# Adjacency product and routed feed-forward on one core: the start, the second expert's loads and the last expert's rows rearranged

## The chip, the cores and the metric

The kernel runs on one core of a Trainium2 chip. The metric is the device time of one execution in microseconds (us); less is better. Engines are named as the profile names them: PE is the matrix engine (PEld its weight loads), DVE the vector engine, ACT the scalar engine, POOL is GpSimd, SP the engine that issues most DMAs (SPq is its queue). Times inside a trace count from the span's start.

## The reference

```python
def _L0_gnn_ref(user_feat, item_feat, adj, W_item, b_item, W_user, b_user):
    h = item_feat @ W_item.T + b_item            # items: 10000 x 128
    b = user_feat @ W_user.T + b_user
    return jax.nn.relu(adj @ h + b)              # adj: 10000 x 10000, 400 MB
...
x = x + _L0_gnn_ref(_layernorm(x, axis=-1), ...)
# feed-forward: layernorm, logits = x @ gate_w + gate_b, softmax, argmax -> one of 8 experts;
# each expert keeps its first C = 1250 * 1.25 = 1563 tokens in order of arrival;
# hmid = relu(buf @ w1 + b1); ybuf = hmid @ w2 + b2; y = ybuf[slot] * prob, 0 for tokens not kept
x = x + _L0_ffn_ref(_layernorm(x, axis=-1)[None], ...)[0]
```

## The kernel before

**Adjacency part.** The 10000 users are cut into 20 blocks of 500 (`BLOCK`), the 10000 items into 78 chunks of 128 and a rest of 16 rows. Chunks go in 20 groups (`SIZES`, 4 chunks each, the last 3). For each group SP loads 128 x 2000 floats of the adjacency (`raw`, a ring of 10, 1 MB a group), ACT rounds it to the matrix engine's reduced format (`a_hi`, `high` at L545, a ring of 4), DVE subtracts to get the rest (`a_lo`, `low` at L746), and PE makes per chunk three products: high part of h by `a_hi` (L1210), low part of h by `a_hi` (L1212), high part of h by `a_lo` (L1221). `high_part(b, q, g)` holds the first two kinds, `low_part` the third, one group later.

**h itself** is made during block 0: `h_chunks(g)` on PE (L1193, float32), `h_bias(g)` on DVE (L724, from PSUM), `h_high(g)` on ACT (L531), `h_low(g)` on DVE (L736). PE runs `h_chunks(g + 2)` ahead of `high_part(0, 0, g)`, and needs `h_hi` and `h_lo` of group g for it. DVE runs `low(g)`, `h_low(g + 1)`, `h_bias(g + 2)` in this order; ACT runs `high(g)`, `h_high(g + 1)`. SP loads the items of group g + 2 behind the adjacency of group g, and waits for `h_chunks(g)` there; what stands behind in SP's queue waits with it.

**Start.** SP loads the constants (`cst`, 302.5 KB), then `item_consts` (the item weights, 128 KB), then items. DVE makes a number of small constants (`set_up` counts to 8), PE multiplies the gate's weights by a matrix of 1/128 (L1347, its mean), DVE subtracts the result (L1013), and only then does PE begin with `h_chunks(0)`.

**Routing.** While block b is multiplied, DVE picks the experts of block b - 2 (`choose`, `pick`, `assign`, `settle`), POOL takes a reciprocal root (`x1_scale` at L1103, `x_scale` at L1099, both on 125 x 4 numbers), and issues indirect DMAs: `scatter` (four of 125 rows, L1111, into the experts' slots `records`) and `pass_on` (L1117).

**Feed-forward.** Each expert's slots go in units of tiles x rows (`RANK_UNITS`): 4, 3, 3 and 3 tiles of mostly 124 rows for the first ranks; 31 units with 101 tiles in all. For unit n: SP loads its records (`load_rec`, a ring of `BODY` = 8), ACT normalizes (`normalize_slots`, L636), PE transposes (`turn_slots`, L1305), ACT and DVE split into high and low, PE multiplies by w1 (`mid`, L1317 to L1319) and w2 (`second`, L1328), ACT adds the bias (`take_y`, L663), PE transposes back (`turn_y`, L1339), DVE scales and adds (`gate_and_add`), and POOL writes each tile to `out` with one indirect DMA (L1178). SP learns from DVE which expert comes next (`order_ready`) and which units need the last block's tokens (`landed`, a value load), and loads w1 (`load_w1`, L451) and w2 (`load_w2`, L457) of each expert. The order around the change is written out by hand: the first units are lines of their own, the rest a loop `step(at)` with fixed lags.

## Time and profile before

| what | value |
|---|---|
| median of 3 runs | 1350.68 us (1349.1 to 1350.9) |
| the profiled execution's own time | 1349.38 us |
| its span | 1347.6 us |
| PE busy | 1308.6 us (97%) |
| DVE busy | 1179.6 us (88%) |
| ACT busy | 941.7 us (70%) |
| POOL busy | 533.2 us (40%) |
| DMA, mean over the span | 328 GB/s |

The span runs from the first to the last recorded instruction; the execution's own time is 1.8 us longer. PE's busy time is modelled from pipelined matmuls, so two products that follow each other at once overlap in it: the pace is read from starts, not from durations.

### The profile page before, as it was taken

How to read it: one execution, taken by the hardware profiler on the slowest of the kernel's cores; microseconds unless marked ns; L12 is line 12 of the kernel's file. 1: busy time of each engine (PE TensorE's matmuls, PEld its weight loads, DVE VectorE, ACT ScalarE, POOL GpSimd, SP SyncE). 2: the span in 40 equal slices, each digit the busy share in tenths (PEclk: the TensorE clock that was granted, in tenths of full speed). 3: DMA queues.
4: the chain of work that ended last, by engine and by line, in shares of the span. 5: the costliest groups of instructions: out<-in, count | busy, mean ns of one | idle time of the engine just before them, and what ended most of it. 6: DMA issues, size and time to landing. Idle time of an engine off the chain costs nothing. (4 is left out here: it accounts for less than half of the span.)

```text
span 1347.6 us, 19376 instructions
## 1 busy us (share of the span) xinstructions
PE 1308.6 (97%) x6026; PEld 1077.9 (80%) x6026; DVE 1179.6 (88%) x1828; ACT 941.7 (70%) x918; POOL 533.2 (40%) x332
## 2 busy tenths in 40 slices
PE   7999999999999999999999999999999999799993
PEld 6888888888888888888888888888888888577772
DVE  7999989898898998989989899898898988577774
ACT  4777767767677676776767768767677676587771
POOL 0001063250431514415134052350532636777887
PEclk9999999999999999999999999999999999899997
DMA  8999999999999999999999999999999995343310
GB/s 322 358 379 407 413 399 398 375 378 386 366 381 370 374 392 367 381 377 371 386 366 376 380 375 374 378 373 385 370 378 379 368 369 226 102 113 91 78 46 4
DMA packets 96743, 441.52 MB, mean 328 GB/s; under 512 B 26601, under 2 KB 34551, under 8 KB 96695
## 3 DMA queue, kind: packets, MB, share of 16 engines
q1 hardware_dynamic: 68815, 417.83, 81.3%
q0 software_dynamic: 21920, 12.86, 3.8%
q10 hardware_dynamic: 5960, 10.24, 2.3%
q8 instruction: 24, 0.39, 0.1%
q14 instruction: 24, 0.20, 0.0%
HBM read 427.77 MB, written 23.83 MB: 335 GB/s over the span
## 5 line engine op out<-in xcount | busy, mean ns | idle before, releaser
L746 DVE TENSOR_TENSOR a_lo<-raw,a_hi 128x2000 fp32r<-128x2000 f32 (+1 forms) x400 | 864.0, 2187 | 76.3 <-ACT a_hi L545 74.4
L545 ACT CAST a_hi<-raw 128x2000 fp32r<-128x2000 f32 (+1 forms) x400 | 724.0, 1827 | 272.6 <-PE bank L1212 170.9
L1210 PE MATMUL bank<-a_hi,h_hi 128*128 128x500 f32 x1560 | 613.3, 393 | 0.7 <-issue 0.7
L1212 PE MATMUL bank<-a_hi,h_lo 128*128 128x500 f32 x1560 | 606.0, 388 | 0.0
L1221 PE MATMUL bank<-a_lo,h_hi 128*128 128x500 f32 x1560 | 418.1, 389 | 0.0
L1210 PEld LDWEIGHTS bank<-a_hi,h_hi 128*128 128x128 f32 x1560 | 293.5, 188 | 59.1 <-issue 1.3
L1221 PEld LDWEIGHTS bank<-a_lo,h_hi 128*128 128x128 f32 x1560 | 293.2, 188 | 58.9
L1212 PEld LDWEIGHTS bank<-a_hi,h_lo 128*128 128x128 f32 x1560 | 294.0, 188 | 56.7
L1103 POOL TENSOR_TENSOR late<-ve,neghalf 125x4 f32<-125x4 f32 x20 | 55.3, 2765 | 620.1 <-DVE ve L763 620.1
L1178 POOL DMA_INDIRECT out<-raw x101 | 138.8, 1374 | 42.0 <-issue 31.3
L1117 POOL DMA_INDIRECT out<-late,kept_out x76 | 134.7, 1772 | 23.1 <-issue 23.1
L1111 POOL DMA_INDIRECT records<-late,slot x80 | 134.2, 1678 | 22.9 <-issue 22.9
L1328 PE MATMUL bank<-raw 128*128 128x372 f32 (+5 forms) x248 | 90.3, 507 | 0.9 <-ACT raw L663 0.9
L1328 PEld LDWEIGHTS bank<-raw 128*128 128x128 f32 x248 | 45.7, 194 | 28.9 <-issue 15.4
L1099 POOL TENSOR_TENSOR xrs<-xve,neghalf 125x4 f32<-125x4 f32 x20 | 28.9, 1446 | 93.6 <-DVE xve L763 93.2
L655 ACT ACTIVATE raw<-bank,raw 128x372 f32<-128x372 f32 (+5 forms) x124 | 63.6, 592 | 1.6 <-PE bank L1319 1.3
L636 ACT ACTIVATE raw<-raw 124x128 f32<-124x128 f32 (+4 forms) x101 | 42.2, 492 | 7.0 <-DMA raw<-records 7.0
L663 ACT ACTIVATE raw<-bank,raw 128x372 f32<-128x372 f32 (+5 forms) x31 | 18.3, 592 | 39.2 <-PE bank L1328 37.0
L1317 PE MATMUL bank<-h_lo 128*128 128x372 f32 (+5 forms) x124 | 45.6, 368 | 0.0
L1318 PE MATMUL bank<-h_lo 128*128 128x372 f32 (+5 forms) x124 | 42.7, 344 | 0.0
L1319 PE MATMUL bank<-h_lo 128*128 128x372 f32 (+5 forms) x124 | 42.5, 343 | 0.0
L1041 DVE TENSOR_TENSOR raw<-bank,raw 124x384 f32<-124x384 f32 (+5 forms) x31 | 18.3, 591 | 22.9 <-PE bank L1339 22.6
(147 smaller groups left out, 830.3 us busy)
## 6 DMA issues: line engine op xcount, KB each, us to landing
raw<-adj_m SPq DMA_DIRECT2D x380, 1000.0 KB
raw<-adj_m SPq DMA_DIRECT2D x20, 500.0 KB
xT<-x_t ACTq DMA_DIRECT2D x20, 250.0 KB
late<-items_t SPq DMA_DIRECT2D x19, 256.0 KB, 4.9
xb<-x ACTq DMA_DIRECT2D x20, 224.0 KB
raw<-records SPq DMA_DIRECT2D x14, 191.8 KB
raw<-w SPq DMA_DIRECT2D x8, 258.5 KB
raw<-w SPq DMA_DIRECT2D x8, 256.0 KB
```

Of the source, the lines that this page charges most:

```text
L545: last = nc.scalar.copy(a_hi[:, g % HI_RING, 0:m], raw[:, g % RAW, 0:m])
L655: nc.scalar.activation(hm[:, n % HM_RING, f, 0:m], ps_mid[f][:, 0:m], ACT.Relu, bias=bias_of(n, f)).then_inc(hm_ready, 1)
L746: last = v.tensor_tensor(a_lo[:, g % RAW, 0:m], raw[:, g % RAW, 0:m], a_hi[:, g % HI_RING, 0:m].bitcast(F32), ALU.subtract)
L1103: p.tensor_tensor(rec[:, q, :, C_RSTD:C_RSTD + 1], ve[:, :].unsqueeze(2), neghalf[:, :].unsqueeze(2), ALU.pow).then_inc(rstd_ready, 1)
L1111: p.indirect_dma_start(rec_d, bass.IndirectOffsetOnAxis(ap=slot[:, q, j:j + 1], axis=0), rec[:, q, j, :], None, bounds_check=SLOTS - 1, oo ...
L1117: p.indirect_dma_start(out, bass.IndirectOffsetOnAxis(ap=kept_out[:, q, j:j + 1], axis=0), rec[:, q, j, 0:HID], None, bounds_check=USERS - ...
L1178: p.indirect_dma_start(out, bass.IndirectOffsetOnAxis(ap=tokq[0:slot_rows(n), n % YRING, j:j + 1].bitcast(U32), axis=0), yout[0:slot_rows( ...
L1210: nc.tensor.matmul(acc[q][:, 0:BLOCK], h_hi[:, k * HID:(k + 1) * HID], a, start=(k == 0), stop=False)
L1212: last = nc.tensor.matmul(acc[q][:, 0:BLOCK], h_lo[:, k * HID:(k + 1) * HID], a, start=False, stop=False)
L1221: last = nc.tensor.matmul(acc[q][:, 0:BLOCK], h_hi[:, k * HID:(k + 1) * HID], a_lo[:, g % RAW, c * BLOCK:(c + 1) * BLOCK], start=False, st ...
L1317: nc.tensor.matmul(to, w1_hi[:, w, cols], x2q_hi[:, n % 2, 0:m], start=True, stop=False)
L1328: last = nc.tensor.matmul(ps_y[:, 0:m], wb2[:, w, f * HID:(f + 1) * HID], hm[:, n % HM_RING, f, 0:m], start=(f == 0), stop=(f == FC - 1))
```

## The change

- **Start.** SP loads `item_consts` first and `cst` only behind the items of group 2. The first adjacency group is loaded and rounded in two halves, and PE begins with the first half. PE first makes 8 products of a constant tile (`WARM`) that nothing uses. The small constants, the gate's mean product and its subtraction move into block 0 and block 1.
- **Order in block 0.** PE runs `high_part(0, 0, g)` ahead of `h_chunks(g + 2)`; SP loads the items of group g + 1, not g + 2, behind adjacency group g. `h_low` moves from DVE to POOL.
- **Second expert.** SP loads records of units 4 and 5 ahead of w1 and w2, units 6 and 7 follow, and w1 of the third expert comes behind them, each expert's number loaded when it is needed. `normalize_slots(4)` on ACT stands behind `take_y(2)`, `turn_slots(4)` on PE behind `turn_y(2)`, `gate_and_add(2)` ahead of the loop.
- **Last block.** POOL runs `x1_scale(19)` behind the third of the four scatters of block 18, not behind all four.
- **Last expert.** Its first two units have 124 rows, not 122.

```diff
-RANK_UNITS = (WHOLE,) * 6 + (((4, 124), (3, 124), (3, 124), (2, 125)), ((4, 122), (4, 122), (3, 102)))
+RANK_UNITS = (WHOLE,) * 6 + (((4, 124), (3, 124), (3, 124), (2, 125)), ((4, 124), (4, 124), (3, 102)))
...
+                    half = 2 * BLOCK if fixed and b == 0 and g == 0 else 0
+                    if half:
+                        sp.dma_start(raw[:, 0, 0:half], adj_b[:, 0:half],
+                                     max_dma_last_dim=16384).then_inc(first_half_loaded, 16)
...
-                    if fixed and b == 0 and g + 2 < GROUPS:
-                        load_items(g + 2)
+                    if fixed and b == 0 and 2 <= g + 1 < GROUPS:
+                        load_items(g + 1)
+                        if g == 1:
+                            sp.dma_start(cst[:, :], consts).then_inc(consts_loaded, 16)
...
-            sp.dma_start(cst[:, :], consts).then_inc(consts_loaded, 16)
-            sp.dma_start(gnn[:, 0:2 * HID], item_consts).then_inc(consts_loaded, 16)
+            sp.dma_start(gnn[:, 0:2 * HID], item_consts).then_inc(item_consts_loaded, 16)
...
                     store_last_x1()
                     sp.wait_ge(order_ready, 2)
                     expert.append(sp.value_load(order_rest[0:1, 1:2], min_val=0, max_val=EXPERTS - 1))
-                    load_w1(1)
-                    enough[n] = landed(n)
+                    enough[n] = enough[n + 1] = landed(n + 1)
...
                 load_rec(n)
-                if n == UNITS_E:
+                if n == UNITS_E + 1:
+                    load_w1(1)
                     load_w2(1)
-                    expert.extend(sp.value_load(order_rest[0:1, m:m + 1], min_val=0, max_val=EXPERTS - 1)
-                                  for m in range(2, EXPERTS))
+                if n == BODY - 1:
+                    expert.append(sp.value_load(order_rest[0:1, 2:3], min_val=0, max_val=EXPERTS - 1))
                     load_w1(2)
-                    for m in range(UNITS_E + 1, BODY):
-                        enough[m] = landed(m)
...
+                half = 2 * BLOCK if isinstance(b, int) and b == 0 and g == 0 else 0
+                if half:
+                    act.wait_ge(first_half_loaded, 16)
+                    nc.scalar.copy(a_hi[:, 0, 0:half], raw[:, 0, 0:half]).then_inc(first_half_hi, 1)
...
+            def set_up_consts():
+                dve.wait_ge(users_done, 1)
+                v.tensor_copy(tok[:, :, :].rearrange("p a j -> p (a j)"), const("tok", TP)).then_inc(set_up, 1)
...
                     low(b, g)
-                    if fixed and b == 0 and g + 1 < GROUPS:
-                        h_low(g + 1)
                     if fixed and b == 0 and g + 2 < GROUPS:
                         h_bias(g + 2)
+                    if fixed and b == 0 and g == 2:
+                        clear_packed()
+                    if fixed and b == 0 and g == 6:
+                        split_users()
+                    if fixed and b == 1 and g == 1:
+                        set_up_consts()
+                    if fixed and b == 1 and g == 4:
+                        centre_gate()
...
+            def h_low(g):
+                pool.wait_ge(h_hi_ready, g + 1)
+                a, n = FIRST[g] * HID, SIZES[g] * HID
+                m = n - HID if g == GROUPS - 1 else n
+                last = p.tensor_tensor(h_lo[:, a:a + m], h_raw[:, a:a + m], h_hi[:, a:a + m].bitcast(F32), ALU.subtract)
...
+                else:
+                    for g in range(2, GROUPS):
+                        h_low(g)
...
-            pool.wait_ge(set_up, 8)
+            pool.wait_ge(set_up, 2)
+            h_low(0)
+            h_low(1)
             x_scale(0)
             blocks(pool, body)
-            scatter(BLOCKS - 2, 0)
+            scatter(BLOCKS - 2, 0, range(0, 3))
             x1_scale(BLOCKS - 1, 1)
+            scatter(BLOCKS - 2, 0, range(3, TILES))
             pass_on(0)
...
                 for g in range(GROUPS):
+                    high_part(b, q, g)
                     if fixed and b == 0 and g + 2 < GROUPS:
                         h_chunks(g + 2)
-                    high_part(b, q, g)
+                    if fixed and b == 1 and g == 3:
+                        gate_mean()
...
+            pe.wait_ge(set_up, 1)
+            for _ in range(WARM):
+                nc.tensor.matmul(ps_x[0:TP, 0:TP], one[:, 0:1].broadcast_to([TP, TP]),
+                                 one[:, 0:1].broadcast_to([TP, TP]), start=True, stop=True)
+            pe.wait_ge(item_consts_loaded, 16)
             h_chunks(0)
...
-            turn_slots(4)
             second(3)
             turn_y(2)
+            turn_slots(4)
```

In the order rows below, names are those of the code: `late<-items_t` is the load of an item group, `raw<-adj_m` of an adjacency group. DVE at the program's start, before, from its second small constant on:

```order
L1011 MEMSET colsT 128x128
L1013 TENSOR_TENSOR cst<-cst,bank 128x8
L724 TENSOR_TENSOR h_raw<-bank,gnn 128x512
L736 TENSOR_TENSOR h_lo<-h_raw,h_hi 128x512
L724 TENSOR_TENSOR h_raw<-bank,gnn 128x512
L757 BN_STATS xst<-xb 125x6 x4
...
L746 TENSOR_TENSOR a_lo<-raw,a_hi 128x2000
L736 TENSOR_TENSOR h_lo<-h_raw,h_hi 128x512
L724 TENSOR_TENSOR h_raw<-bank,gnn 128x512
```

and DVE there in the change, from its second instruction on:

```order
L1038 MEMSET neghalf 125x4
L743 TENSOR_TENSOR h_raw<-bank,gnn 128x512 x2
L766 BN_STATS xst<-xb 125x6 x4
...
L755 TENSOR_TENSOR a_lo<-raw,a_hi 128x2000
L743 TENSOR_TENSOR h_raw<-bank,gnn 128x512
```

DVE has no subtraction for `h_lo` any more between two adjacency groups; those stand at POOL's start, where nothing but `x_scale` stood before:

```order
L1124 TENSOR_TENSOR h_lo<-h_raw,h_hi 128x512 x2
L1134 TENSOR_TENSOR xrs<-xve,neghalf 125x4
L1124 TENSOR_TENSOR h_lo<-h_raw,h_hi 128x512 x17
L1124 TENSOR_TENSOR h_lo<-h_raw,h_hi 128x256
L1126 TENSOR_TENSOR h_lo<-h_raw,h_hi 16x128
```

SP where the second expert begins, before (`records` of 124x528 is unit 4, `w` of 128x512 is w1, of 128x517 w2; a TENSOR_LOAD is a value load):

```order
L491 TENSOR_LOAD clear_runs
...
L451 DMA raw<-w 128x512
L443 TENSOR_LOAD landed_at
...
L472 DMA raw<-records 124x528
...
L457 DMA raw<-w 128x517
L499 TENSOR_LOAD clear_runs
...
L451 DMA raw<-w 128x512
L443 TENSOR_LOAD landed_at
...
L472 DMA raw<-records 124x396
```

and in the change:

```order
L502 TENSOR_LOAD clear_runs
...
L454 TENSOR_LOAD landed_at
...
L483 DMA raw<-records 124x528
...
L483 DMA raw<-records 124x396
...
L462 DMA raw<-w 128x512
...
L468 DMA raw<-w 128x517
...
L483 DMA raw<-records 124x396
```

Unit 4's records lose one weight load ahead of them; unit 5's (124x396) lose all three and, with six loads of experts' numbers and three of `landed_at`, nine value loads.

## Rows read from the trace of the kernel before

**Rows 1.** Busy time by stretch: start:end, then length, each engine, PE clock, DMA share.

```profile
80.00:90.00 10.00, 9.34 (x41) 7.44 (x41) 9.61 (x16) 7.13 (x7) 2.93 (x1) 1.00 0.83 320
200.00:1100.00 900.00, 899.88 (x4096) 750.81 (x4095) 823.97 (x1164) 646.48 (x494) 313.24 (x177) 1.00 1.00 377
1150.00:1200.00 50.00, 41.63 (x188) 31.02 (x189) 33.67 (x105) 33.56 (x75) 34.62 (x28) 0.93 0.40 109
```

**Rows 2.** Timeline of the start: start, duration, engine, instruction, idle before.

```profile
0.74 0.42 SPq L432 DMA_DIRECT2D cst<-consts  x1
2.62 0.43 SPq L414 DMA_DIRECT2D raw<-adj_m  x1
5.41 0.17 DVE L1000 COPY tok<-cst 125x8 f32<-125x8 f32 x1 [4.50 <-DMA gnn<-item_consts]
7.78 3.78 PE L1193 MATMUL bank<-gnn,late 128*128 128x128 f32 x16 [0.26 <-DVE cst L1013]
9.97 0.69 DVE L724 TENSOR_TENSOR h_raw<-bank,gnn 128x512 f32<-128x512 f32 x1 [2.25 <-PE bank L1193]
10.26 0.43 SPq L414 DMA_DIRECT2D raw<-adj_m  x1
10.70 0.62 ACT L531 CAST h_hi<-h_raw 128x512 fp32r<-128x512 f32 x1 [4.99 <-DVE h_raw L724]
14.42 0.77 PE L1210 MATMUL bank<-a_hi,h_hi 128*128 128x500 f32 x1
15.23 1.86 ACT L545 CAST a_hi<-raw 128x2000 fp32r<-128x2000 f32 x1 [1.64 <-DMA raw<-adj_m]
```

**Rows 3.** Timeline of block 0: PE's first product of two groups, DVE's round.

```profile
21.64 0.47 PE L1210 MATMUL bank<-a_hi,h_hi 128*128 128x500 f32 x1
24.08 2.23 DVE L746 TENSOR_TENSOR a_lo<-raw,a_hi 128x2000 fp32r<-128x2000 f32 x1
25.27 0.47 PE L1210 MATMUL bank<-a_hi,h_hi 128*128 128x500 f32 x1
26.23 0.68 DVE L736 TENSOR_TENSOR h_lo<-h_raw,h_hi 128x512 fp32r<-128x512 f32 x1
26.83 0.68 DVE L724 TENSOR_TENSOR h_raw<-bank,gnn 128x512 f32<-128x512 f32 x1
```

**Rows 4.** POOL's own arithmetic: one line's durations (ns min/median/max), groups with mean ns.

```profile
L1103 POOL TENSOR_TENSOR late<-ve,neghalf x20: 1021/2964/2966, 114.3 to 1151.2; 125x4 f32<-125x4 f32 x20
L390 POOL TENSOR_TENSOR carrier_pool<-one 125x1 f32<-125x1 f32 x20 | 23.7, 1185 | 6.5 <-DMA records<-h_raw,clear_edge 6.5
L1124 POOL MEMSET h_raw<- 125x1848 f32 x1 | 1.7, 1652 | 0.0
```

**Rows 5.** Timeline between the adjacency part and the feed-forward, single rows.

```profile
1149.99 1.19 POOL L1111 DMA_INDIRECT records<-late,slot  x1 [0.30 <-issue]
1151.20 1.06 POOL L1103 TENSOR_TENSOR late<-ve,neghalf 125x4 f32<-125x4 f32 x1
1154.90 0.27 PE L1269 MATMUL bank<-run,one_r 125*125 125x8 f32 x1 [2.67 <-DVE run L826]
1162.91 0.02 SPq L472 DMA_DIRECT2D raw<-records  x1
1168.11 1.65 ACT L636 ACTIVATE raw<-raw 124x128 f32<-124x128 f32 x4 [3.06 <-DMA raw<-records]
1169.87 1.37 SPq L472 DMA_DIRECT2D raw<-records  x3
1176.21 0.54 PE L1305 MATMUL bank<-cst,raw 124*128 124x124 f32 x3 [1.44 <-ACT raw L636]
```

**Rows 6.** Timeline of POOL at the end of the span.

```profile
1315.86 1.32 POOL L1178 DMA_INDIRECT out<-raw  x1 [0.30 <-issue]
1324.79 1.68 POOL L1178 DMA_INDIRECT out<-raw  x1 [1.31 <-DVE raw L1059]
1339.28 1.67 POOL L1178 DMA_INDIRECT out<-raw  x1 [0.30 <-issue]
```

More of the change, by code:

```diff
@@ L544, in high @@
                 m, n = full_cols(g), group_cols(g)
-                last = nc.scalar.copy(a_hi[:, g % HI_RING, 0:m], raw[:, g % RAW, 0:m])
+                last = nc.scalar.copy(a_hi[:, g % HI_RING, half:m], raw[:, g % RAW, half:m])
                 if m < n:
@@ L1078, in _ @@
             slots_low(4)
+            gate_and_add(2)
             def step(at):
@@ L1084, in step @@
                     slots_low(at - LAG_IN)
-                if has(at, LAG_OUT):
+                if has(at, LAG_OUT, EARLY + 1):
                     gate_and_add(at - LAG_OUT)
@@ L1104, in x1_scale, with scatter @@
                                 neghalf[:, :].unsqueeze(2), ALU.pow).then_inc(rstd_ready, 1)
-            def scatter(m, q):
-                wait_on_pool(pool, slots_ready, m + 1, q)
-                for j in range(TILES):
+            def scatter(m, q, tiles_of=range(TILES)):
+                if tiles_of[0] == 0:
+                    wait_on_pool(pool, slots_ready, m + 1, q)
+                for j in tiles_of:
                     p.indirect_dma_start(rec_d, bass.IndirectOffsetOnAxis(ap=slot[:, q, j:j + 1], axis=0),
```

96 lines of the change are left out of this document (55 added, 41 removed).

## The prediction

> **What bounds the kernel now.** I read the busy time by stretch first. From 200 to 1100 us PE is busy for 899.88 of 900.00 us, so the adjacency part is PE's, and what comes early at its start stays early at its end [rows 1]. Two other stretches show a hole: 80 to 90 us (9.34 of 10.00) and 1150 to 1200 us (41.63 of 50.00). Then I read the timeline at three places.
>
> At the start PE does nothing useful until 7.78: DVE has waited until 5.41 for both constant loads, and small constants and the gate's mean stand ahead of PE's first item product [rows 2]. The first adjacency product starts at 14.42, the second group is late again, because its load was issued only at 10.26 (ACT sits idle until it lands and rounds from 15.23). The first 16 passes of item products take 3.78, some 0.22 each.
>
> In block 0 a group takes PE 25.27 - 21.64 = 3.63, and DVE's round runs from 24.08 to 26.83 + 0.68 = 27.51, 3.43 [rows 3]. PE leads, DVE is close behind.
>
> Between the parts PE waits for the last block's routing (until 1154.90) and for the second expert's records (until 1176.21), and after that it has no long idle time; POOL's writes to `out` follow it and end the span [rows 5, 6].
>
> **The change part by part.**
>
> *Start.* The item weights go first. Both constant loads are there at 5.41 today [rows 2]; without the 302.5 KB of `cst` I put the first items at 4.4 (they are 256 KB behind 128 KB). The 8 unused products are 16 passes of some 0.21, from 0.9 to 4.3: they hide under the loads. Then: item products of group 0, 8 passes at 0.21, to 6.1; DVE's bias 0.69, to 6.9; ACT's rounding 0.62, to 7.6 [rows 2]; the half group's cast, half of 1.86, to 8.5; POOL's subtraction beside it to 8.8. PE starts on the adjacency at 8.9 and not 14.42: -5.5. Adjacency group 1 is now issued at some 3.0, not 10.26, lands at 10.2 behind the 1 MB of group 0, and is rounded by 12.0.
>
> *The subtraction on POOL.* No row shows POOL subtracting 512 numbers from 512. Bounds: not below DVE's 0.68 [rows 3]; from above, POOL fills 1848 numbers in 1.652, 0.89 ns each [rows 4], so three streams of 512 one after another are 1.37, with 0.2 to start 1.6. I take 1.2, between the two. The second question is whether DVE and POOL can work side by side. The same POOL instruction on 125 x 4 numbers takes 1.02 at its shortest and 2.964 in the median [rows 4], and by the code's order it becomes ready just as DVE's 2.23 subtraction begins: POOL waits for it to end, and then takes its own time. So a round on DVE is its 2.15 (start to next start: 26.23 - 24.08), then POOL's 1.2 with the bias (0.60) beside it: 3.35, still under PE's 3.63. It takes PE's place as the bound from 1.48 upwards. In steady state it costs nothing; in the first groups it does. `h_low(1)` and `low(0)` become ready together at about 10.1; if DVE goes first, POOL ends at 13.4 and PE starts group 1 at 13.5. Group 2 comes behind `low(1)` (to 15.6), POOL's reciprocal root (1.05) and `h_low(2)` (1.2): 17.9, against 21.64 today [rows 3]: -3.7. From there both run at PE's pace, and I carry -3.7 through block 0.
>
> The Trainium skill (SBUF — State Buffer, "SBUF: two separate sides" and "Who interferes with whom") says that GpSimd and a DVE instruction with two SBUF inputs exclude each other for the whole instruction, whichever came first. The trace agrees for POOL behind DVE (1.02 against 2.964). By another page (GPSIMD Engine Reference, "Elementwise — side-by-side cycle accounting") a two-input element costs POOL 2.6 cycles at 1.2 GHz, an estimate of 1.1 for 512; the sum would be the same within 0.3.
>
> *Small moves.* The hole at 80 to 90 (0.66 lost, where PE needs the last `h_low`, which DVE does behind `low(18)`) closes, since POOL does it at once: -0.6. The gate's mean comes back as one product inside block 1: +0.25. Five small constants on DVE in block 1 are some 0.9 in a block where DVE has 8% to spare (823.97 of 900) [rows 1]; without that cover they would cost 0.9. Start in sum: -3.7 - 0.6 + 0.25 = **-4.0**, bounds -5.7 (POOL grants first) and 0 (POOL at 1.6, below).
>
> *Last block.* `x1_scale(19)` starts at 1151.20, behind the fourth scatter (1149.99); behind the third it starts at 1149.7: -1.5 for routing on DVE, for PE's wait until 1154.90, and for the order that SP waits for [rows 5]. The fourth scatter comes 1.1 later, with nobody waiting for it before the last blocks' `pass_on`, which starts as today.
>
> *Second expert.* Unit 4's records are issued at 1162.91 and normalized at 1168.11, 5.2 later, with two weight loads around them; unit 5's are issued at 1169.87, and PE gets them at 1176.21 [rows 5]. In the change unit 4's are issued at about 1161.0 (-1.5, and a weight load's issue less), unit 5's right behind. I take 4.2 for the first (without w1 in front) and 2.3 more for the second: 1165.2 and 1167.5; w1 behind them 1168.4. ACT then splits w1 (0.6), rounds unit 4 (0.6) and normalizes unit 5 (three quarters of 1.65): 1170.9. PE's `turn_slots(5)` and `mid(4)` start at 1171.0 and not at 1176.21: **-5.2**. In the meantime PE does `second(3)` and `turn_y(2)`, which no longer stand behind unit 4. Unit 6's records wait for the last scatter (issued at 1163, landed near 1167) and are there near 1171.5; PE wants them at 1174. From there on PE leads as before, and POOL keeps up: it still waits for DVE ahead of an expert's first unit (1.31 at 1324.79) [rows 6]. Bounds: -1.5 (only the earlier root counts) and -6.5.
>
> *Last expert.* A write to `out` of 124 rows takes 1.32 + 0.30 = 1.62 (the row at 1315.86); the eight of 122 rows run from 1324.79 to 1339.28 + 1.67 + 0.30 = 1341.25: 16.46, 2.06 each [rows 6]. POOL is alone on the path there. With 124 rows they take 8 x 1.62 = 12.96: **-3.5**. The 8 columns more in two units cost PE 8 of 488, +0.1.
>
> **Sum.** -4.0 - 5.2 - 3.5 + 0.1 = -12.6. Against the profiled execution's own 1349.38 that is 1336.8; this execution lay 1.3 under the median of the runs, 1350.68, so I say 1338.1.
>
> **Rivals.**
> 1. *POOL is slow in block 0* (1.6 a subtraction). Each of 18 groups loses 1.6 - 1.48 = 0.12, some 2.2, and the first ones 1.0 more: the start's gain falls to about -1. For it: the upper bound of the rows; against it: the pages. 1341.
> 2. *The records don't come early.* If the loads of units 4 and 5 share what limits them, or unit 5 or w1 lands as late as unit 5 today, the piece is worth 1.5. For it: unit 4's load alone needs 5.2; against it: unit 5 isn't even issued until 1169.87. 1341.8.
> 3. *The slow writes aren't due to 122 rows* but to what runs at the end. For it: the row at 1324.79 is beside DVE's work. Against it: the one at 1339.28 is as slow, when little else runs. 1341.6.
> 4. *Slower.* POOL's subtraction takes as long as its median 2.96, and each waits for DVE and DVE for it. A round is then 2.15 + 2.96 = 5.1 and not 3.63, 19 times: +28, so -12.6 becomes +16: 1366. It decides from a subtraction of 1.48 + 12.6 / 19 = 2.14 on. Against it: 2.96 holds a wait of 2; alone the instruction takes 1.02.
> 5. *More than forecast*: POOL gets in ahead of `low(0)`, PE's clock rises during the unused products: the start is -5.7. 1336.4.
>
> **How the numbers follow.** The forecast 0.55 (own range 1336.5 to 1340), rival 1 0.13, rival 2 0.12, rival 3 0.05, rival 5 0.08, rival 4 0.04; 0.03 that several parts fail and nothing is left. Range 1334.5 to 1344: it leaves out rival 4, and room below for a transition of -6.5 with rival 5, above for two of the rivals 1 to 3 together. 0.2% (2.7 us) is about what a measurement of this kernel can tell from no change. Faster 0.92, same 0.04, slower 0.04.
>
> **What the profile of the change would show.** PE's first adjacency product near 8.9, that of group 2 near 17.9, of block 1's first group some 4 earlier than today; POOL's 20 subtractions of 1.2, recorded up to 3.4 where they wait; `x1_scale(19)` 1.5 closer to the third scatter; PE's long waits before units 4 and 5 shrunk to one of 2 to 3; the last eight 4-tile writes 1.62 apart. Wrong it would be made by a POOL subtraction over 1.5, by records of unit 5 that land later than 6 after unit 4's issue, or by writes of 124 rows that stay 2.0 apart.

## The result and the profile after

The changed kernel takes 1343.76 us (median of 6 runs, 1343.03 to 1344.92), the kernel before 1349.24 beside it (6 runs, 1348.1 to 1350.9): ratio 0.9959, 95% interval 0.9949 to 0.997. That is 5.5 us less where 12.6 had been summed. The profiled executions say the same, 1343.59 against 1349.38 us, spans 1341.8 against 1347.6.

Busy time of the changed kernel in the stretches of [rows 1] (start:end, length, PE, PEld, DVE, ACT, POOL, PE clock, DMA share, GB/s):

```profile
80.00:90.00 10.00, 9.06 (x40) 7.24 (x40) 9.69 (x8) 6.88 (x6) 4.58 (x3) 1.00 0.75 292
200.00:1100.00 900.00, 899.84 (x4095) 750.79 (x4094) 824.36 (x1167) 646.21 (x495) 316.58 (x177) 1.00 1.00 377
1150.00:1200.00 50.00, 43.31 (x203) 32.64 (x204) 36.41 (x113) 34.72 (x79) 36.13 (x30) 0.97 0.41 113
```

The long middle is as full as before. The stretch from 80 to 90 us, whose hole was to close, has a larger one (9.06 against 9.34), and the transition has 1.7 us more of PE's work in it.

The timeline of the changed kernel's start, which answers to [rows 2, 3] (start, duration, engine, instruction, idle before):

```profile
5.12 2.19 PE L1235 MATMUL bank<-gnn,late 128*128 128x128 f32 x16 [0.48 <-DMA late<-items_t]
7.89 1.26 POOL L1124 TENSOR_TENSOR h_lo<-h_raw,h_hi 128x512 fp32r<-128x512 f32 x1 [7.46 <-ACT h_hi L541]
9.42 0.47 PE L1257 MATMUL bank<-a_hi,h_hi 128*128 128x500 f32 x1 [2.11 <-ACT a_hi L551]
...
12.62 1.16 PE L1235 MATMUL bank<-gnn,late 128*128 128x128 f32 x8 [0.86 <-DMA late<-items_t]
14.03 0.47 PE L1257 MATMUL bank<-a_hi,h_hi 128*128 128x500 f32 x1 [0.26 <-POOL h_lo L1124]
16.43 1.16 PE L1235 MATMUL bank<-gnn,late 128*128 128x128 f32 x8 [0.34 <-DMA late<-items_t]
18.34 0.39 PE L1257 MATMUL bank<-a_hi,h_hi 128*128 128x500 f32 x1
20.14 1.05 PE L1235 MATMUL bank<-gnn,late 128*128 128x128 f32 x8
22.02 0.47 DVE L798 TENSOR_SCALAR h_hi<-cst 32x128 fp32r<-32x128 f32 x2
22.53 2.24 DVE L755 TENSOR_TENSOR a_lo<-raw,a_hi 128x2000 fp32r<-128x2000 f32 x1
22.72 3.19 POOL L1124 TENSOR_TENSOR h_lo<-h_raw,h_hi 128x512 fp32r<-128x512 f32 x1 [0.97 <-ACT h_hi L541]
26.02 0.47 PE L1257 MATMUL bank<-a_hi,h_hi 128*128 128x500 f32 x1 [0.28 <-issue]
```

The reader is to see that the first steps came nearly as worked out: the first adjacency product 5.0 us earlier than before (9.42), the third group's 3.3 earlier (18.34 against 21.64), the subtraction alone 1.26 on POOL. Beside DVE's `low` the same subtraction is recorded with 2.5 to 3.2. The last five rows are the hand-over of which much is made below: the item products of group 4 (20.14), the clearing (22.02), `low` behind it (22.53), POOL's subtraction, which ends at 25.91, and PE's first product of group 4 at 26.02, where the pace of 3.6 us a group would have had it at 25.6.

The head start did not last. This table follows PE's first product of a group, changed minus before, from the two timelines:

| group of block 0 | 0 | 2 | 3 | 4 | 7 | 13 | 14 | 17 | 18 | 19 | block 1, group 6 on |
|---|---|---|---|---|---|---|---|---|---|---|---|
| us | -5.0 | -3.31 | -3.31 | -2.87 | -2.32 | -2.35 | -1.95 | -1.96 | -1.11 | -0.83 | -0.62 |

The difference of 0.6 us then stays to the end of the adjacency part. The rows at groups 7, 14 and 19:

```profile
33.92 1.65 ACT L585 ACTIVATE rows<-xb,xnb,xrs 125x128 f32<-125x128 f32 x4
35.47 1.85 ACT L559 CAST a_hi<-raw 128x2000 fp32r<-128x2000 f32 x1
37.46 0.47 PE L1257 MATMUL bank<-a_hi,h_hi 128*128 128x500 f32 x1 [0.37 <-ACT a_hi L559]
...
59.61 0.67 DVE L791 TENSOR_TENSOR xlT_lo<-bank,xlT_hi 128x500 fp32r<-128x500 f32 x1
60.43 3.15 POOL L1124 TENSOR_TENSOR h_lo<-h_raw,h_hi 128x512 fp32r<-128x512 f32 x1 [1.06 <-ACT h_hi L541]
...
80.12 3.60 DVE L755 TENSOR_TENSOR a_lo<-raw,a_hi 128x2000 fp32r<-128x2000 f32 x2
80.14 2.52 POOL L1126 TENSOR_TENSOR h_lo<-h_raw,h_hi 16x128 fp32r<-16x128 f32 x1
82.76 0.47 PE L1257 MATMUL bank<-a_hi,h_hi 128*128 128x500 f32 x1 [0.94 <-issue]
```

The last three explain the hole: the last group's subtraction is two instructions, and the second, of 16 rows only, began 0.02 us after DVE's `low` and took 2.52. PE starts 0.10 behind its end. (In e9 below, the same instruction stands behind the end of `low` and takes 0.45.)

The transition of the changed kernel, which answers to [rows 5], from the timelines of POOL, PE, SP and ACT:

```profile
1149.32 1.04 POOL L1138 TENSOR_TENSOR late<-ve,neghalf 125x4 f32<-125x4 f32 x1
1153.01 0.27 PE L1319 MATMUL bank<-run,one_r 125*125 125x8 f32 x1 [1.37 <-DVE run L860]
1160.01 0.86 SPq L483 DMA_DIRECT2D raw<-records  x2
1166.37 1.65 ACT L654 ACTIVATE raw<-raw 124x128 f32<-124x128 f32 x4 [1.25 <-DMA raw<-records]
1169.44 0.62 ACT L646 CAST h_lo<-raw 128x512 fp32r<-128x512 f32 x1 [1.42 <-DMA raw<-w]
1171.74 0.54 PE L1363 MATMUL bank<-cst,raw 124*128 124x124 f32 x3 [3.03 <-ACT raw L654]
1176.39 0.48 PE L1363 MATMUL bank<-cst,raw 124*128 124x124 f32 x3
```

`turn_slots(5)` came at 1171.74 instead of 1176.21. But the next one, which followed after 3.08 us before (1179.29), followed after 4.65. The windows of the changed kernel over this place say why (the last three figures are PE's granted clock, DMA share, GB/s):

```profile
1170.00:1172.00 2.00, 0.26 (x2) 0.26 (x3) 1.88 (x4) 1.69 (x5) 1.70 (x2) 1.00 0.39 90
1172.00:1174.00 2.00, 2.00 (x9) 1.63 (x8) 1.92 (x6) 0.47 (x1) 1.43 (x2) 0.61 0.87 228
1174.00:1176.00 2.00, 2.00 (x7) 1.62 (x6) 1.12 (x4) 1.91 (x5) 1.66 (x2) 0.54 0.64 217
```

PE had idled for 3.03 us, then its clock was at the lower level of 1.2 GHz for 3.4 us (1172.4 to 1175.8), just under `mid(4)`. In the kernel before, a stretch of the same length lay at 1170.1, ahead of the wait of 1.44 us in front of `turn_slots(5)`, which hid it. At the first unit of the fourth expert (`turn_slots(12)`) PE is at 1209.80, before 1212.86: -3.06, of which -0.6 is the start's. The transition gave 2.4.

POOL at the end, to be set against [rows 6]:

```profile
1322.30 1.32 POOL L1220 DMA_INDIRECT out<-raw  x1 [2.00 <-DVE raw L1083]
1333.80 1.32 POOL L1220 DMA_INDIRECT out<-raw  x1 [0.30 <-issue]
1335.43 1.12 POOL L1220 DMA_INDIRECT out<-raw  x1 [0.30 <-issue]
```

The eight 4-tile writes take 1335.43 - 1322.30 = 13.13 instead of 16.46: -3.3. PE and DVE bring the first of them 2.49 earlier, 0.6 less than PE's 3.06 (0.15 for the added columns, 0.4 on DVE). In sum -0.62 - 2.44 - 2.71 = -5.77, the difference of the spans.

### The profile page after: what moved, and what is told of

It reads as the page before. It is cut to its first block and busy times, and to the rows that moved or that the text cites. A ratio compares the mean times of both kernels' runs of the same rounds, so it can differ in the third digit from the quotient of the medians.

```text
span 1341.8 us, 19460 instructions
## 1 busy us (share of the span) xinstructions
PE 1309.0 (98%) x6042; PEld 1076.6 (80%) x6042; DVE 1171.4 (87%) x1807; ACT 941.1 (70%) x920; POOL 582.2 (43%) x353
## 5 line engine op out<-in xcount | busy, mean ns | idle before, releaser
L1220 POOL DMA_INDIRECT out<-raw x101 | 135.0, 1337 | 40.4 <-issue 30.4
L1386 PE MATMUL bank<-raw 128*128 128x372 f32 (+4 forms) x248 | 88.0, 496 | 1.6 <-ACT raw L681 1.6
L673 ACT ACTIVATE raw<-bank,raw 128x372 f32<-128x372 f32 (+4 forms) x124 | 63.4, 592 | 1.9 <-PE bank L1377 1.8
L1124 POOL TENSOR_TENSOR h_lo<-h_raw,h_hi 128x512 fp32r<-128x512 f32 (+1 forms) x20 | 50.3, 2516 | 28.4 <-ACT h_hi L541 27.6
L681 ACT ACTIVATE raw<-bank,raw 128x372 f32<-128x372 f32 (+4 forms) x31 | 18.4, 593 | 40.1 <-PE bank L1386 40.1
L1375 PE MATMUL bank<-h_lo 128*128 128x372 f32 (+4 forms) x124 | 46.0, 371 | 0.0
L654 ACT ACTIVATE raw<-raw 124x128 f32<-124x128 f32 (+3 forms) x101 | 42.3, 492 | 2.9 <-DMA raw<-records 2.9
L1377 PE MATMUL bank<-h_lo 128*128 128x372 f32 (+4 forms) x124 | 43.2, 348 | 0.0
L1376 PE MATMUL bank<-h_lo 128*128 128x372 f32 (+4 forms) x124 | 43.1, 348 | 0.0
L594 ACT CAST xlT_hi<-bank 128x500 fp32r<-128x500 f32 x20 | 11.5, 575 | 36.8 <-PE bank L1286 36.8
```

The costliest lines, as they stand in the source:

```text
L673: nc.scalar.activation(hm[:, n % HM_RING, f, 0:m], ps_mid[f][:, 0:m], ACT.Relu, bias=bias_of(n, f)).then_inc(hm_ready, 1)
L1220: p.indirect_dma_start(out, bass.IndirectOffsetOnAxis(ap=tokq[0:slot_rows(n), n % YRING, j:j + 1].bitcast(U32), axis=0), yout[0:slot_rows( ...
L1375: nc.tensor.matmul(to, w1_hi[:, w, cols], x2q_hi[:, n % 2, 0:m], start=True, stop=False)
L1377: nc.tensor.matmul(to, w1_hi[:, w, cols], x2q_lo[:, n % 2, 0:m], start=False, stop=True).then_inc(mid_done, 1)
L1386: last = nc.tensor.matmul(ps_y[:, 0:m], wb2[:, w, f * HID:(f + 1) * HID], hm[:, n % HM_RING, f, 0:m], start=(f == 0), stop=(f == FC - 1))
```

## The experiments

Eighteen runs. Times are medians; "ratio" is to the kernel before, with its 95% interval. One microsecond is 0.07%, and the intervals are some 0.13% to either side, so pieces under 2 us are read from the traces. Two places in a trace serve as marks: PE's first product of block 1, group 6 ("start" below is its distance to the kernel before's, which is at 102.4 us), and `turn_slots(5)`.

| run | time | ratio | start |
|---|---|---|---|
| e1_hlow_dve | 1343.96 | 0.9965 (0.9951-0.9978) | -1.75 |
| e2_chunks_first | 1344.48 | 0.9967 (0.9955-0.9979) | -0.63 |
| e3_both | 1344.25 | 0.9963 (0.9949-0.9977) | -0.27 |
| e4_rows124 | 1346.63 | 0.9983 (0.9974-0.9992) | -0.67 |
| e5_chunks_first_from4 | 1342.02 | 0.9941 (0.9927-0.9954) | -1.59 |
| e6_from4_dve | 1343.61 | 0.9950 (0.9936-0.9963) | -1.46 |
| e7_fill | 1345.44 | 0.9964 (0.9950-0.9977) | -0.26 |
| e8_w1_between | 1344.32 | 0.9950 (0.9936-0.9964) | -0.38 |
| e9_moved | 1342.93 | 0.9955 (0.9942-0.9969) | -0.88 |
| e10_dve_moved | 1343.19 | 0.9955 (0.9941-0.9968) | -1.75 |
| e11_fill12 | 1344.11 | 0.9961 (0.9947-0.9975) | -0.79 |
| e12_weights_first | 1344.81 | 0.9964 (0.9952-0.9977) | -1.00 |
| e13_x1_whole | 1345.02 | 0.9970 (0.9958-0.9982) | -1.82 |
| e14_before_sp | 1347.59 | 0.9990 (0.9980-1.0000) | -0.57 |
| e15_dve_fill | 1343.04 | 0.9959 (0.9946-0.9973) | -1.87 |
| e16_dve_w1_fill | 1343.34 | 0.9963 (0.9949-0.9976) | -2.50 |
| e17_changed_again | 1343.61 | 0.9952 (0.9938-0.9965) | -0.76 |
| e18_from4_again | 1342.37 | 0.9944 (0.9931-0.9958) | -2.27 |

The last column must be read with its own spread: e4 and e14 have the kernel before's start, and lie at -0.67 and -0.57; the changed kernel's start stands in the changed kernel (-0.62), e7, e8, e11, e12, e13 and e17, from -0.26 to -1.82, mean -0.80. Like for like the changed start is worth 0.80 - 0.41 = 0.4 us, from seven traces against three, and less than the spread of either. The spread is nearly all there at the fourth group of block 0 (20.79 us in e13, 22.33 in e7). What is lost from group to group behind it repeats: in all seven traces some 0.45 at group 4 and 0.40 at group 14. So a single start says little, and these losses say much.

### The start

**e1_hlow_dve.** The subtraction goes back to DVE:

```diff
                     low(b, g)
+                    if fixed and b == 0 and g + 1 < GROUPS:
+                        h_low(g + 1)
```

> The changed kernel with one part undone: the low part of h is subtracted on DVE again, behind each group's low, as before the change. Theory A (in block 0 a loop of two groups runs from PE's high_part through h_chunks, h_bias, h_high and POOL's subtraction, which cannot start while DVE's low runs, and has no slack against PE's 7.25 us): the POOL hop of about 1.3 us goes, some 0.6 us of DVE work comes in, so most late inputs are absorbed; the first product of block 1 comes 2 to 3 us earlier than in the kernel before instead of 0.6, time about 1341.9 us. Theory B (late transfers of adjacency and constants eat the head start, whoever subtracts): block 1 stays at 0.6 us earlier, 1343.8 us. Theory C (DVE was the bound in block 0 and POOL relieves it): PE falls behind, 1345 us or more.

Measured: start -1.75, 1.1 more than the changed kernel's trace; e15 and e16, which have the same start, lie at -1.87 and -2.50, against the -0.80 that is the mean with POOL. The losses at group 4 (0.45) and group 14 (0.40) are gone, that at group 7 stayed, and 0.4 was lost at group 19. Between A and B; C is out. The median did not show it.

**e2_chunks_first** and **e3_both.** PE's order inside a group goes back, alone and together with e1's edit:

```diff
-                    high_part(b, q, g)
                     if fixed and b == 0 and g + 2 < GROUPS:
                         h_chunks(g + 2)
+                    high_part(b, q, g)
```

> The changed kernel with PE's h_chunks(g + 2) put ahead of high_part(g) again, as before the change; POOL still subtracts. Theory A (two-group loop without slack): the chunks start one high_part, 1.8 us, earlier, the loop has 1.8 us of slack, block 1 begins about 3 us earlier than in the kernel before, time about 1341.3 us. Rival A2 (POOL's stretched subtraction of 2.5 us itself makes each high_part wait, wherever the chunks stand): no change, 1343.8 us. Theory B (late transfers): no change, 1343.8 us.

> The changed kernel with both undone: the low part of h on DVE and h_chunks(g + 2) ahead of high_part(g). What stays of the start is the early items and the half groups. Theory A: all waits of block 0 but the late transfers are gone, block 1 begins 3 to 4 us earlier than in the kernel before, time 1340.5 to 1341.5 us. Theory B: no change from the changed kernel, 1343.8 us. Theory C (DVE is the bound in block 0 without POOL's help): block 1 about where it was before or later, 1344 us or more.

PE in e2, start of the timeline:

```profile
5.08 2.47 PE L1235 MATMUL bank<-gnn,late 128*128 128x128 f32 x16 [0.44 <-DMA late<-items_t]
12.72 2.00 PE L1235 MATMUL bank<-gnn,late 128*128 128x128 f32 x8 [5.18 <-DMA late<-items_t]
14.38 0.77 PE L1257 MATMUL bank<-a_hi,h_hi 128*128 128x500 f32 x1
```

Both forecasts of 1341 missed, and the rows show why: with the chunks ahead PE waits 5.18 us for the third group's items, and the whole head start is gone before the first product. But from there PE keeps 3.62 a group to group 17 (4.09 at group 9 and 4.3 at group 15, as before), and the 0.8 ahead of group 19 are gained, with POOL's subtraction recorded as long as ever. So the slow POOL rows cost next to nothing by themselves: they cost where the order leaves them no room. (The times of e2 and e3 are no measure of the start: in the transition of e2's trace the clock was low twice, in e3's for 6.8 us.) In this order group 18 follows group 17 by 2.84, as before; in the changed order by some 3.67, in every run. That is the last group's item products (0.83): in the changed order they stand behind `high_part(17)` and not ahead of it. The table above counts them as head start up to group 17, and they are none.

**e5_chunks_first_from4** and **e6_from4_dve.** The changed order up to group 3, that of before from group 4 on, with the subtraction on POOL or on DVE:

```diff
+                    if fixed and b == 0 and 4 <= g < GROUPS - 2:
+                        h_chunks(g + 2)
                     high_part(b, q, g)
-                    if fixed and b == 0 and g + 2 < GROUPS:
+                    if fixed and b == 0 and g < 4:
                         h_chunks(g + 2)
```

> The changed kernel with h_chunks(g + 2) ahead of high_part(g) from group 4 on only; groups 0 to 3 keep the changed order, POOL still subtracts. It separates what the two runs before mixed: the order with the chunks ahead cost the 5 us head start because PE's first chunks wait for the third group's items, but kept PE's pace of 3.62 us afterwards. Theory A (the loop of two groups has no slack in the changed order): the head start of about 3 us that is left at group 4 stays to group 17, and the wait ahead of group 19 goes, so that block 1 begins 3 to 3.7 us earlier than in the kernel before; time 1341 us. Theory B (the transfers run out: block 0 moves 1.29 MB a group at a DMA share of 0.96 to 1.00): PE cannot be that far ahead, it loses 2 us on late inputs again, block 1 begins 0.6 to 1 us earlier, 1343.8 us.

> The same order as in the run before, and the low part of h subtracted on DVE again. Theory A with the lock as its cause: with 1.8 us of slack in the loop it hardly matters who subtracts: block 1 begins 3 to 3.7 us earlier, as in the run before, 1341 us. Theory C (DVE, busy 3.8 of every 4 us in block 0, is the bound once PE is ahead): DVE's round of 3.6 us or more lets PE fall back to 1.7 us earlier, as in the run with the subtraction on DVE alone, 1342.5 us.

PE's first wait for items at the change of order, in e5, then in e6:

```profile
30.32 1.16 PE L1235 MATMUL bank<-gnn,late 128*128 128x128 f32 x8 [0.65 <-DMA late<-items_t]
```

```profile
27.10 1.16 PE L1233 MATMUL bank<-gnn,late 128*128 128x128 f32 x8 [1.54 <-DMA late<-items_t]
```

Both forecasts fell between: -1.6 and -1.5. The change of order meets items that have not landed (some 1.9 us lost over groups 4 and 5 in e5, 2.6 at group 4 in e6, 0.8 of it the item products that now stand ahead), and afterwards little is lost, 0.43 at group 16 in e5 and 0.2 at group 10 in e6, while the hole at group 19 closes (0.8). By the start, who subtracts no longer matters here, as A said. The 1.6 us between the two medians do not speak against it: the two profiled executions lie 1.75 apart, and 1.6 of it arise in the transition, where the clock is low for 3.4 us in e5 and for 6.8 in e6. e5's 1342.02 is the lowest of the first sixteen runs.

**e9_moved** and **e10_dve_moved.** Two pieces of DVE's work go elsewhere, the subtraction on POOL or on DVE:

```diff
-                    if fixed and b == 0 and g == 2:
+                    if fixed and b == 0 and g == 18:
                         clear_packed()
...
-                    if g == 17 and (not fixed or b < BLOCKS - 1):
+                    if g == (18 if fixed and b == 0 else 17) and (not fixed or b < BLOCKS - 1):
```

> The changed kernel with two pieces of DVE work moved to group 18 of block 0: the clearing of the packed rows (0.47 us, from group 2) and the variance of the second block's x (1.4 us, from group 17). Nothing else differs. Theory A (in the changed order the loop of two groups has no slack, so each extra piece of DVE work in block 0 goes straight into PE): the loss of 0.45 us at group 4 and that of 0.85 us at group 18 are gone, and block 1 begins 1.8 to 2.2 us earlier than in the kernel before, not 0.6: 1342.3 us. Theory B (the transfers of items and adjacency set PE's place by the end of block 0): the same losses come at other groups, block 1 stays at 0.6 us earlier, 1343.8 us.

> As the run before, and the low part of h is subtracted on DVE again. With the subtraction on DVE alone PE kept 3.1 us of its head start to group 17 and lost 1.2 us at groups 18 and 19, just where the variance of x stands. Theory A: with the variance behind h_low(19) nothing is lost there, block 1 begins 2.8 to 3.1 us earlier than in the kernel before: 1341.2 us, the best start of all. Theory C (DVE is full in block 0, 3.8 of every 4 us, so the work only moves the loss): block 1 begins 1.7 us earlier, as without the move, 1342.7 us.

Half right. Without the clearing group 4 loses nothing (0.45 in the changed kernel), so that piece did go straight into PE. The 0.84 at group 18 stayed, though the variance had left: they are the item products of above, and I had read them wrongly. At group 19 PE waits 0.17 in e9 and not 0.94 (without the variance ahead of it `low(18)` begins at 78.42 and not 80.12, and POOL is done at 81.66), but the moved work comes back as 0.77 at block 1's group 2, where DVE is still behind:

```profile
81.76 0.46 PE L1257 MATMUL bank<-a_hi,h_hi 128*128 128x500 f32 x1 [0.17 <-issue]
...
88.59 1.17 PE L1268 MATMUL bank<-a_lo,h_hi 128*128 128x500 f32 x4 [0.50 <-DVE a_lo L755]
```

In e10 the same happened with 1.0, and it ended where e1 did, as its Theory C said. DVE is full around the end of block 0, and moving its work by one group does not make it less.

### The last expert

**e4_rows124.** The kernel before with `(4, 124), (4, 124), (3, 102)` as its last units.

> The kernel before with one part of the change alone: the two 4-tile units of the last expert have 124 rows instead of 122. If the rows make POOL's eight writes shorter (the changed kernel's trace has 13.1 us for eight against 16.5), the time is 2.8 us less: 3.3 less in the eight writes, 0.2 more columns on PE, about 0.3 more on DVE: 1346.4 us. If the writes were short in the changed kernel for another reason (its other order, other traffic), they stay near 2.06 us each and the time is 1349.3 us.

```profile
1325.39 1.32 POOL L1178 DMA_INDIRECT out<-raw  x1 [2.01 <-DVE raw L1059]
1336.89 1.32 POOL L1178 DMA_INDIRECT out<-raw  x1 [0.30 <-issue]
1338.52 1.12 POOL L1178 DMA_INDIRECT out<-raw  x1 [0.31 <-issue]
```

The first theory held: eight writes take 13.13 again, in a kernel that differs in nothing else, and the time is 2.4 us less. Rival 3 of the prediction is out.

### The transition

**e12_weights_first.** SP's order of the weights and records goes back, the rest stays:

```diff
+                    load_w1(1)
                     enough[n] = enough[n + 1] = landed(n + 1)
...
-                if n == UNITS_E + 1:
-                    load_w1(1)
+                if n == UNITS_E:
                     load_w2(1)
-                if n == BODY - 1:
                     expert.append(sp.value_load(order_rest[0:1, 2:3], min_val=0, max_val=EXPERTS - 1))
                     load_w1(2)
```

> The changed kernel with one part undone: on SP the second expert's w1 is issued ahead of the records again, and its w2 and the third's w1 behind its first record load, as before the change. It sizes the reordering of the loads by itself. Theory W (the early record loads are what brings turn_slots(5) from 1176.2 to 1171.7 us): turn_slots(5) comes at 1175 us or later and the time is 2 to 3 us more than the changed kernel's, 1346.5 us. Rival V (the earlier x1_scale and the order of ACT, DVE and PE did it, and the loads land early enough either way): turn_slots(5) at 1172 us, no change, 1343.8 us.

`turn_slots(5)` came at 1172.02, 0.65 later than in the changed kernel once the start is taken off. Rival V was near, and the order that the change is named after is worth 0.7 in this pair of traces. The SP rows of e12 show what else it had changed: the record loads of units 5 to 7 are issued from 1163.29 on, where the kernel before came to unit 5's only at 1169.87, behind six reads of experts' numbers, w1 of the third expert and the landing counts. The kernel before:

```profile
1162.99 0.36 SPq L457 DMA_DIRECT2D raw<-w  x1
1167.05 0.34 SPq L451 DMA_DIRECT2D raw<-w  x1
```

Between these two issues stand the six reads, and 3.7 us pass. In e12 one read stands there, and 0.97 pass.

**e14_before_sp.** The kernel before with SP's part of the change alone.

> The kernel before with SP's part of the feed-forward alone changed: the records of the second expert's first two units ahead of its weights, one landing count for both, and the experts' numbers read one at a time instead of six together. The order on PE, ACT and DVE is that of before. Theory S (the six reads and the landing counts ahead of the fifth unit's record load, which was issued at 1169.9 us, made it late): it is issued near 1163 us, ACT's normalize_slots(5) no longer waits for it, but PE still has turn_slots(4) ahead of second(3), so turn_slots(5) comes at 1174.5 to 1175 us instead of 1176.2: 1347.8 us. Rival R (the record loads only share the engines with the weights and land at the same time): 1349.3 us.

SP and PE in e14:

```profile
1161.64 0.86 SPq L472 DMA_DIRECT2D raw<-records  x2
...
1173.78 0.49 PE L1338 MATMUL bank<-cst,raw 128*124 128x128 f32 x3
1174.11 0.48 PE L1304 MATMUL bank<-cst,raw 124*128 124x124 f32 x3
```

As forecast: both record loads issued together, `turn_slots(5)` right behind `turn_y(2)` with no wait, at 1174.11, and the time 1347.59 (forecast 1347.8; the kernel before beside it 1348.82, and the interval just reaches 1.0, so the gain in time is not shown by the medians alone).

**e13_x1_whole.** `x1_scale` behind all four scatters again:

```diff
-            scatter(BLOCKS - 2, 0, range(0, 3))
+            scatter(BLOCKS - 2, 0)
             x1_scale(BLOCKS - 1, 1)
-            scatter(BLOCKS - 2, 0, range(3, TILES))
```

> The changed kernel with one part undone: POOL's x1_scale of the last block stands behind all four scatters of the block ahead of it again, not behind three. Theory X (POOL's chain of the clearing, the scatters and x1_scale sets the routing of the last block): the fourth scatter's 1.5 us comes ahead of x1_scale, PE's count products come 1.5 us later against the last adjacency product, and where the longer idle time makes the clock fall as well up to 3.5 us later; time 1345.3 us or more. Rival: DVE's own chain is late anyway and hides it, 1343.8 us.

PE in e13:

```profile
1152.96 0.37 PE L1318 MATMUL bank<-run,one_r 125*125 125x8 f32 x1 [2.53 <-DVE run L860]
```

Theory X held in the trace; the time, 1345.02, is just under its 1345.3 and no more than 1.3 above the changed kernel's, with overlapping intervals. From POOL's first scatter to `x1_scale` there are 11.80 us and not 10.38. The wait for the routing is 2.53 and not 1.37, the count products come 1.2 later once the start is taken off, and they take 0.37 and not 0.27: the clock had fallen, and stayed at the lower level from 1151.4 to 1158.2.

**e8_w1_between.** w1 between the two record loads:

```diff
+                if n == UNITS_E:
+                    load_w1(1)
                 if n == UNITS_E + 1:
-                    load_w1(1)
                     load_w2(1)
```

> The changed kernel with the second expert's w1 issued between its first and second record load instead of behind both. Theory W (ACT's wait of 1.42 us for w1 sets turn_slots(5) at 1171.7 us, because the split stands ahead of normalize_slots(5)): w1 lands some 1.5 us earlier and turn_slots(5) comes 0.8 to 1.2 us earlier, time 1342.8 us. Rival R (the transfers share the same engines: the second record load lands as much later as w1 lands earlier, and normalize_slots(5) waits for it instead): turn_slots(5) within 0.3 us of before, 1343.8 us; if the records of 1584 bytes a packet go slowest at the end, up to 1 us later, 1344.8 us.

ACT no longer waits for w1, and PE's wait ahead of `turn_slots(5)` is 1.82. But the routing had come 1.1 later in this execution and the clock was low from 1153.3 to 1160.1, so that `turn_slots(4)` was 2.0 late and the loads had that much more time. The run says nothing on w1's place; the time (1344.32) shows no gain.

**e7_fill** and **e11_fill12.** Products without use keep PE busy in its wait:

```diff
             turn_y(2)
             turn_slots(4)
+            for _ in range(12):
+                nc.tensor.matmul(ps_mid[0][:, 0:HID], ident, ident, start=True, stop=True)
```

> The changed kernel with 22 products of the identity with itself, written to a bank that mid(4) overwrites, between turn_slots(4) and turn_slots(5), where PE waits 3.03 us. They do no work of the kernel. Theory K (the granted clock falls from 1172.4 to 1175.8 us because PE stood idle, and the cold mid(4) costs 1.5 us): the clock stays at 1.0 there, turn_slots(5) to turn_slots(6) takes 3.1 us instead of 4.65, and the rest comes 1.5 us earlier: 1342.2 us. Rival K2 (the clock falls for the idle time ahead of it, at about 1164 and 1158 us, whatever PE does in this wait): no change of the clock, and the fill delays turn_slots(5) by up to 0.5 us: 1343.8 to 1344.3 us.

> The changed kernel with filling products on PE that do no work of the kernel: 12 between turn_slots(4) and turn_slots(5), where PE waits 3.0 us (one takes 0.23 us, as the run with 22 showed, which were too many), and 4 ahead of total, where PE waits 1.4 us for the last block's routing. Theory K (PE's idle time in the transition lets the clock fall, once or twice, and each fall costs 1.6 to 2.5 us where PE is the bound): no stretch under 1.0 between 1150 and 1180 us, turn_slots(5) to turn_slots(6) 3.1 us, and the time 1.6 us less than the changed kernel's, 1342.2 us. Rival K2 (the clock falls as often as before, since the waits ahead of 1150 us bring it): one cold stretch stays, 1343.8 us or up to 1 us more.

In e7 I had the price of a product wrong: the 22 were to fit the wait of 3.03 us, took 5.08 and pushed `turn_slots(5)` to 1176.19. With 12 (and 4 ahead of `total`) they took 2.85. In both the clock stayed at 1.00 at this place, and the following distance fell from 4.65 to 3.02 and 3.58. Theory K is right on the clock and wrong on the time: no gain that can be measured in either.

**e15_dve_fill** and **e16_dve_w1_fill** combine e1 with the filling products, e16 with e8's edit too.

> A combination: the changed kernel, the low part of h on DVE again (it began block 1 1.75 us earlier than the kernel before, the changed kernel 0.62), and 12 filling products between turn_slots(4) and turn_slots(5) (no low clock there, 1.1 us). The filling products do no work of the kernel. Theory A and K together: 1.1 us from the start and 1.1 us from the clock, 1341.6 us. Rival (the clock or the routing's landing times move by 1 us from run to run and hide it): 1342.5 to 1343.8 us.

> As the run before, with w1 issued between the two record loads (in that run PE's wait ahead of turn_slots(5) was 1.82 us instead of 3.03) and 8 filling products instead of 12, since the wait is shorter. Theory: 1.1 us from the start, 1.1 from the clock, up to 1.0 from w1: 1340.7 us. Rival: w1 was not the limit there, since turn_slots(4) had come late in that run and gave the loads time; nothing over the run before, 1341.6 us.

ACT, then PE in e15:

```profile
1173.56 1.27 ACT L654 ACTIVATE raw<-raw 124x128 f32<-124x128 f32 x3 [1.55 <-DMA raw<-records]
```

```profile
1170.97 0.54 PE L1361 MATMUL bank<-cst,raw 124*128 124x124 f32 x3 [1.06 <-ACT raw L654]
1174.90 0.51 PE L1361 MATMUL bank<-cst,raw 124*128 124x124 f32 x3 [0.70 <-ACT raw L654]
```

Here is where the clock's gain goes. `mid(4)` at full clock is done by 1174.2, but unit 6's records are there only at 1173.56 and PE waits 0.70 for them to be normalized. The low clock had hidden that landing. Of e16 the same holds (a wait of 0.69). The rivals held in what they said of the mechanism: 1343.04 and 1343.34, no gain over e1 (1343.96) that can be measured; e16's number, 1341.6, was missed.

**e17_changed_again** and **e18_from4_again**, on one chip: the changed kernel and e5 once more.

> The changed kernel itself once more, to see what one execution of it differs from the next. By the six traces with the same start, PE's block 1 begins 0.3 to 1.8 us earlier than in the profile of before, 0.8 on the mean; time 1343.8 us, ratio 0.996.

> The order with h_chunks(g + 2) ahead of high_part(g) from group 4 on once more, on the same chip as the changed kernel. If its gain is the kernel's (the switch of order costs 2 us at groups 4 and 5, then PE keeps its pace and the wait ahead of group 19 goes): block 1 begins 1.3 to 1.9 us earlier than in the profile of before and the time is 0.8 to 1.7 us less than the changed kernel's. If the first run of it was a lucky set: no difference, 1343.8 us.

e17 came as forecast, start -0.76 and 1343.61 (1342.76 to 1344.6). e18: 1342.37 (1341.57 to 1342.71). The five times of e18 lie below all five of e17. The order with the chunks first from group 4 on beats both kernels, the changed one by some 1.2 us; its trace has the start at -2.27, earlier than the forecast's 1.3 to 1.9.

## Why the prediction was wrong

Its range held the time and its signs were right, but the change was worth less than half of the sum.

**The start, -4.0 forecast, -0.6 measured (-0.4 like for like).** The step that failed is "From there both run at PE's pace, and I carry -3.7 through block 0". POOL's subtraction was not at fault: 1.26 against 1.2. Four things were:

- The mark was badly chosen. -3.31 at group 2 was read at the first product of the group, and the change moves some 0.8 of item products from ahead of it to behind it. The gain in work done was some 2.5. Shown by group 18, which comes some 3.67 behind group 17 in every run of the changed order and 2.83 to 2.84 behind it in the runs with the chunks ahead (3.05 in e14).
- The round on DVE is not all there is. In the changed order there is a chain over two groups: `high_part(g)`, item products, `h_bias`, ACT's rounding, POOL's subtraction (held until `low` ends), `high_part(g + 2)`. It has next to no room, so that each extra piece goes into PE: the clearing (0.45; the sum had no term for it), ACT's normalization of x (0.53), DVE's `xlT_lo` (0.40), 1.4 in sum. Shown for the clearing by e9, and for the order by e2, which has all three pieces and loses 0.15. For the other two pieces the rows at groups 7 and 14 say it; no run moved them. That 0.85 of it come from POOL's place in that chain is shown by e1, e15 and e16, which lose nothing at groups 4 and 14.
- The hole at group 19 did not close (-0.6) but grew by 0.28. The last subtraction is two instructions, and the second met `low(18)`. I had the lock in the argument and did not look at which instructions of DVE it would meet there.
- The items of the third and fourth group land late (PE waits 0.86 and 0.34 for them in the changed kernel), and group 2 comes at 18.34 and not at 17.9, 0.4 of the -3.7. How late differs from execution to execution: e13, with the same code there, had its third group 1.2 us ahead of the changed kernel's.

The gate's mean cost 0.21 inside block 1, close to the 0.25 forecast.

The Trainium skill (SBUF — State Buffer, "SBUF: two separate sides") has GpSimd and a DVE instruction with two SBUF inputs exclude each other for a whole instruction. The rows agree: 1.26 alone, 2.56 in the median beside `low`, and for the one of 16 rows 2.52 behind the start of `low` and 0.45 behind its end (e9).

**The transition, -5.2 forecast, -2.4 measured.** The direction and the place were right, and `x1_scale` is worth about the 1.5 that was said (from the first scatter to it 10.38 us in the changed kernel, 11.80 in e13). `turn_slots(5)` came 3.9 earlier. What was off was the landing: unit 4 was ready 1.8 later than forecast and w1 1.7, both once the start is taken off. Then 1.4 were given back under `mid(4)`, through the low clock or, without it, through unit 6's records (e15): "From there on PE leads as before" was the step. And I gave the credit to the order of records and weights; by e12 and e14 it is the six reads and the counts on SP that had held up unit 5's load. The size moves from execution to execution: the ten traces with the changed transition (the changed kernel, e1, e2, e3, e5, e6, e9, e10, e17, e18) give 1.1 to 3.1 at `turn_slots(12)`, 2.1 in the mean, and e4, with the transition of before, lies 0.7 behind the kernel before. In e17 and e2 the routing came 1.1 later and the transition was worth 1.2 only; in e3 and e6 the routing was in time, but the low clock lasted 6.8 us and not 3.4, and it was worth 1.1 and 1.5. In e17 most of it stands on POOL, which waited 7.49 us for its clearing writes to land and not 6.62; what decides that landing stayed open.

**The last expert, -3.4 forecast, -2.7 measured.** The eight writes nearly as forecast (-3.3 against -3.5); 0.15 for columns and 0.4 on DVE, one instruction of which took twice its time, came on top.

Rivals: 1 had the right size (start -1) for a wrong reason; 2 was right that the records would be late, not that they would not come; 3, 4 and 5 did not come.

## What to carry to other kernels

A head start is worth what is left of it where the next bound begins. Read it at a mark that the change does not move against the work, and follow it to the end of the stage before it goes into a sum. Where two engines hand work on in a loop, add up the whole loop with its waits, not the work of each engine: a chain that fits with nothing to spare turns every small instruction beside it into lost time, and an order that leaves one step of room (e5) brings it back. When a stall shrinks, price what lands next; two gains in a row at one place are seldom both paid out.

## What the runs showed of the hardware

- An indirect write of 4 tiles' rows to `out` takes 1.62 us a piece with 124 rows and 2.06 with 122, in the same place of the same kernel (e4): more rows, less time.
- A subtraction of 16 rows of 128 on POOL took 2.52 us where it began 0.02 behind a DVE subtraction of 128x2000, and 0.45 where it began behind its end (e9).
- After an idle time of 3.0 us PE's clock was at its lower level for 3.4 us; in e13 it fell within a wait of 2.5 us and stayed there for 6.8 us; filling products in the wait kept it at the upper one in all four runs that had them at that place, and none of these was measurably faster than the run without them.
- The same code's start lay between 0.3 and 1.8 us ahead of the kernel before's in seven traces, and most of that spread was there by the fourth group.
- Six reads of a number by SP between two of its DMA issues took 3.7 us, one such read 0.97 (the kernel before, e12).
